# Moving the stationary operands of a float32r matmul chain to odd multiples of 32 bytes, modulo 512, from the moving operands

## The chip, the core and the metric

The kernel runs on one core of one Trainium2 chip. The metric is the device time of one execution in microseconds (us); shown are the median and the ends of three runs, and one further execution that the hardware profiler recorded. The engines are named as in the profile: PE is TensorE's matmuls, PEld its weight loads, DVE is VectorE, ACT is ScalarE, POOL is GpSimd, and SP issues most DMAs.

## The reference

The input x has 4 sequences of 1024 tokens with 1024 features, cut into 8 groups of 128. Everything is float32.

```
h  = einsum('btel,elf->btef', x.reshape(B, T, 8, 128), W1) + b1     # 8 experts, 128 -> 512
h  = gelu(h)
y  = einsum('btef,efl->btel', h, W2) + b2                           # 512 -> 128
eo = silu(cond) @ emb_W + emb_b                                     # one row per sequence
scale, shift = split(eo)
hn = layernorm(y.reshape(B, T, 1024), ln_g, ln_b) * (1 + scale) + shift
out = x + silu(hn) @ out_W + out_b                                  # 1024 -> 1024
```

## The kernel before

**Three products for one.** Every operand of a matmul is split into a high part, rounded to float32r, and a low part, the float32r rest. Each product then takes three matmuls: high by high, low by high, high by low. A matmul loads a stationary block of 128 columns (LDWEIGHTS) and streams a moving block of 512 columns past it. Each of the two halves of a 1024-token tile loads its block again, so loads and matmuls are equal in number.

**First stage (L907 to L946).** 32 items, one for each group g and each tile t of 1024 tokens. An item has four chunks of 128 hidden features. For a chunk, `first` (L928) multiplies a 128-column cut of W1 (stationary) with the transposed input `xT_hi`, `xT_lo` (moving) and `second` (L944) a cut of W2 (stationary) with the gelu's parts `g_hi`, `g_lo` (moving): 12 matmuls for a chunk, 48 for an item. PE runs `first` two chunks ahead of `second`. The parts of W1 and W2 of a group lie in one of `WS = 4` slots of the tensor `W` (slot g % 4, each 8 KB on a partition). ACT and DVE write them (L476, L634; the first group L539 to L654) from `wraw`, which the DMA fills.

**Second stage (L948 to L1021).** 16 pairs p of 128-token tiles. DVE, ACT and POOL take the layer norm of a pair and its silu; `round_s` on ACT (L519) writes the high part `s_hi[p % 2]`, `rest_s` on DVE (L800) the low part `s_lo[p % 2]`. In `project` (L954) the silu parts are the stationary operand, in cuts of 128 tokens, and the output weights `oW_hi`, `oW_lo` the moving one: 48 matmuls for a tile, 96 for a pair. The last tile is done in three pieces of 512, 256 and 256 columns (`project_pieces`, L1004: 24 matmuls of 512 columns and 48 of 256). "Pair 1" in the change stands for the buffers with index 1, which the odd pairs use; the even pairs, the first among them, use index 0.

**Order.** All engine programs are written out by hand and wait on semaphores; no scheduler moves an instruction. PE waits for the writers of its operands (`w_split`, `xhi_done`, `glo_done`, `slo_done`) and for the readers of its results (`y_staged`, `out_ready`).

**Places.** `at(name, shape, offset)` (L128) puts a tensor at a fixed byte of each partition, from `BASE = 33 * 512`. With S0 = 64 KB and R0 = S0 + 21 * 512, the matmuls' operands are placed by these lines:

```
oW_hi = at("oW_hi", [P, G, D], 0, F32R)
W = at("W", [P, WS, 4, FF], R0 + 16 * KB, F32R)
xT_hi = at("xT_hi", [P, 2, TA], R0 + 56 * KB, F32R)
g_hi = at("g_hi", [P, 2, TA], R0 + 80 * KB, F32R)
s_lo0 = at("s_lo0", [P, G, TP], R0 + 8 * KB, F32R)
s_hi1 = at("s_hi1", [P, G, TP], R0 + 16 * KB, F32R)
s_lo1 = at("s_lo1", [P, G, TP], R0 + 24 * KB, F32R)
s_hi0 = at("s_hi0", [P, G, TP], R0 + 124 * KB, F32R)
```

All of them start at multiples of 512 bytes. A stationary cut is 128 columns of 4 bytes, 512 bytes, and a moving half is 2048 bytes, so every operand of every matmul of the data starts at 0 modulo 512.

Of the kernel before, what the change touches and what calls it, by code (L numbers as in the profile page):

```python
# [15 lines left out]
def cond_ffn_program(nc, x, xT, vectors, cond, W1, W2, emb_T, out_W, out_b, out):  # L16
    B, T, D = x.shape
    G, L, FF = W1.shape
    C = FF // P
    NE = emb_T.shape[1]  # L20
    K = emb_T.shape[2]
    KH = K // 2
    TA = 2 * BANK
    NT = B * T // TA
    TP = 2 * P
# [6 lines left out]
    HG = G // 2  # L32
# [12 lines left out]
    WS = 4  # L45
# [12 lines left out]
    EARLY = 2  # L58
# [65 lines left out]
    with ExitStack() as ctx:  # L124
# [30 lines left out]


        emb_out = [at(f"emb_out{k}", [P, HG, K], (16 + 32 * k) * KB) for k in range(2)]
        emb_cols = [emb_out[k] if o is None else at(f"emb_cols{k}", [P, len(range(NE)[cut]), K], R0 + o * KB)
                    for k, (_, cut, o) in enumerate(PIECES)]


        cond_all = [at(f"cond_all{k}", [P, K], o) for k, o in enumerate((R0 + 128 * KB, S0 + 5632))]
        cond_tanh_all = at("cond_tanh_all", [P, EARLY, K], R0 + 104 * KB)
        dot_out = [at(f"dot_out{k}", [P, KH], S0 + 2 * k * KB) for k in range(2)]
        wraw = at("wraw", [P, 2, 2 * FF], R0 + 8 * KB)
        W = at("W", [P, WS, 4, FF], R0 + 16 * KB, F32R)
        xT_raw = at("xT_raw", [P, 2, TA], R0 + 48 * KB)
        xT_hi = at("xT_hi", [P, 2, TA], R0 + 56 * KB, F32R)
        xT_lo = at("xT_lo", [P, 2, TA], R0 + 64 * KB, F32R)
        g_raw = at("g_raw", [P, 2, TA], R0 + 72 * KB)  # L170
        g_hi = at("g_hi", [P, 2, TA], R0 + 80 * KB, F32R)
        g_lo = at("g_lo", [P, 2, TA], R0 + 88 * KB, F32R)
        y_stage = at("y_stage", [P, 2, TA], R0 + 96 * KB)

        yb0 = at("yb0", [P, G, TP], R0)
        tanh0 = at("tanh0", [P, G, TP], R0 + 8 * KB)
        s_lo0 = at("s_lo0", [P, G, TP], R0 + 8 * KB, F32R)
        s_hi1 = at("s_hi1", [P, G, TP], R0 + 16 * KB, F32R)
        s_lo1 = at("s_lo1", [P, G, TP], R0 + 24 * KB, F32R)
        res = at("res", [P, 4, D], R0 + 48 * KB)  # L180
        yb2 = at("yb2", [P, G, TP], R0 + 64 * KB)
        yb1 = at("yb1", [P, G, TP], R0 + 104 * KB)
        sq = at("sq", [P, G, TP], R0 + 112 * KB)
        out_b_all = at("out_b_all", [P, D], R0 + 120 * KB)
        s_hi0 = at("s_hi0", [P, G, TP], R0 + 124 * KB, F32R)
        tail_out = [at(f"tail_out{k}", [P, K], o) for k, o in enumerate((S0, R0 + 32 * KB))]
        tail_cond = at("tail_cond", [P, B - EARLY, K], R0 + 72 * KB)
        tail_cols = [at(f"tail_cols{k}", [P, K], R0 + o * KB) for k, o in enumerate((36, 40, 80, 84, 88, 92))]
        mean_part1 = at("mean_part1", [P, HG, TP], R0 + 124 * KB)
        yb = (yb0, yb1, yb2)  # L190
        s_hi = (s_hi0, s_hi1)
        s_lo = (s_lo0, s_lo1)
# [264 lines left out]
        def _(act):  # L457
# [7 lines left out]
            def round_raw(j):  # L465
                kind, g = LOADS[j]
                act.wait_ge(wraw_landed[j % 2], raw_count(j))
                if kind == "W" and g >= WS:
                    act.wait_ge(s2_done, C * (LAST_ITEM[g - WS] + 1))
                if kind == "O" and g >= HG:  # L470

                    act.wait_ge(emb_dot, 4 * (2 * (g - HG) + 1))
                for h in range(2):
                    half = slice(h * FF, (h + 1) * FF)
                    if kind == "W":
                        nc.scalar.copy(W[:, g % WS, 2 * h], wraw[:, j % 2, half]).then_inc(w_act_rounded, 1)  # L476
# [59 lines left out]
                round_s(0, h)  # L536

            act.wait_ge(w0_landed, 16)
            nc.scalar.copy(W[:, 0, W1_HI, 0:P], wraw[:, 0, 0:P]).then_inc(w0_rounded, 1)  # L539
            act.wait_ge(x0_landed[1], 16)  # L540
            nc.scalar.copy(xT_hi[:, 0, BANK:], xT_raw[:, 0, BANK:]).then_inc(xhi_done, 1)
            act.wait_ge(w1_landed, 16)
            nc.scalar.copy(W[:, 0, W1_HI, P:FF], wraw[:, 0, P:FF]).then_inc(w_rounded, 1)
            act.wait_ge(vec_landed, 16)
            gelu(0)
            gelu(1)
# [66 lines left out]
        def _(dve):  # L613
            nc.vector.memset(eps[:], LN_EPS).then_inc(eps_set, 1)

            def split_raw(j, h):
                kind, g = LOADS[j]
                half = slice(h * FF, (h + 1) * FF)
                raw = wraw[:, j % 2, half]
                if j == 0:  # L620

                    hi, lo = W[:, 0, W2_HI], W[:, 0, W2_LO]
                    dve.wait_ge(w2_landed, 16)
                    nc.vector.tensor_copy(hi, raw).then_inc(w_rounded, 1)
                    dve.wait_ge(w_rounded, 2)
                elif kind == "W":
                    hi, lo = W[:, g % WS, 2 * h], W[:, g % WS, 2 * h + 1]
                    dve.wait_ge(w_act_rounded, 2 * (g - 1) + h + 1)
                else:
                    hi, lo = oW_hi[:, g, half], oW_lo[:, g, half]  # L630
                    if g >= HG:
                        dve.wait_ge(emb_dot, 4 * (2 * (g - HG) + 2))
                    dve.wait_ge(o_rounded, 2 * g + h + 1)
                nc.vector.tensor_tensor(lo, raw, hi.bitcast(F32), ALU.subtract).then_inc(w_split, 1)  # L634
# [2 lines left out]
            dve.wait_ge(x0_landed[0], 16)  # L637
            nc.vector.tensor_copy(xT_hi[:, 0, 0:BANK], xT_raw[:, 0, 0:BANK]).then_inc(x0_hi, 1)
            dve.wait_ge(w0_rounded, 1)
            nc.vector.tensor_tensor(W[:, 0, W1_LO, 0:P], wraw[:, 0, 0:P], W[:, 0, W1_HI, 0:P].bitcast(F32),  # L640
                                    ALU.subtract).then_inc(w0_split, 1)

            def rest_x0(h):
# [5 lines left out]
            rest_x0(0)  # L649
            rest_x0(1)  # L650
            dve.wait_ge(w_rounded, 1)
            nc.vector.tensor_tensor(W[:, 0, W1_LO, P:FF], wraw[:, 0, P:FF], W[:, 0, W1_HI, P:FF].bitcast(F32),
                                    ALU.subtract).then_inc(w_split, 1)
            split_raw(0, 1)  # L654

# [250 lines left out]
        def _(pe):  # L906
            def first(m, low_part=None):  # L907
                n, c = divmod(m, C)
                g = ORDER[n][0]
                cut = slice(c * P, (c + 1) * P)  # L910
                if m == 2:
                    pe.wait_ge(gelu0_half, 1)
                if m >= 3:
                    pe.wait_ge(gelu_done, m - 1)
                parts = [(W1_HI, xT_hi), (W1_LO, xT_hi), (W1_HI, xT_lo)]
                if m == 1:

                    parts = [parts[0], parts[2], parts[1]]
                for k, (w, v) in enumerate(parts):
                    if m == 1 and k == 2:  # L920
                        pe.wait_ge(w_split, 1)
                    if k == 2 and low_part is not None:
                        pe.wait_ge(xlo_done, low_part)
                    for h in range(2):
                        half = slice(h * BANK, (h + 1) * BANK)
                        if (m, k, h) == (2, 0, 1):
                            pe.wait_ge(gelu_done, 1)
                        mm = nc.tensor.matmul(ring(m)[:, half], W[:, g % WS, w, cut], v[:, n % 2, half],  # L928
                                              start=(k == 0), stop=(k == 2))
                mm.then_inc(s1_done, 1)  # L930

            def second(m):
                n, c = divmod(m, C)
                g = ORDER[n][0]
                cut = slice(c * P, (c + 1) * P)
                if c == 0 and n >= 2:
                    pe.wait_ge(y_staged, n - 1)
                pe.wait_ge(ghi_act if act_rounds(m) else ghi_dve, ROUNDED[m])
                for k, (w, v) in enumerate(((W2_HI, g_hi), (W2_LO, g_hi), (W2_HI, g_lo))):
                    if k == 2:  # L940
                        pe.wait_ge(glo_done, m + 1)
                    for h in range(2):
                        half = slice(h * BANK, (h + 1) * BANK)
                        mm = nc.tensor.matmul(y_psum(n)[:, half], W[:, g % WS, w, cut], v[:, m % 2, half],  # L944
                                              start=(c == 0 and k == 0), stop=(c == C - 1 and k == 2))
                mm.then_inc(s2_done, 1)  # L946

# [17 lines left out]
            for k, h in ((0, 0), (1, 0), (0, 1), (1, 1), (2, 0), (2, 1)):  # L965
# [7 lines left out]
                    pe.wait_ge(w0_split, 1)  # L973
                if k == 2:
                    pe.wait_ge(xlo_done if h else x0_lo, 1)
                mm = nc.tensor.matmul(ring(0)[:, half], W[:, 0, w, 0:P], v[:, 0, half],  # L976
                                      start=(k == 0), stop=(k == 2))
            mm.then_inc(s1_done, 1)
            pe.wait_ge(w_rounded, 1)
# [76 lines left out]
```

## Time and profile before

| | us |
|---|---|
| median of three runs (lowest, highest) | 706.69 (706.60, 706.92) |
| the profiled execution | 707.23 |
| its span, first to last instruction | 705.2 |
| PE busy, 3100 matmuls | 701.7 |
| PEld busy, 3100 loads | 579.7 |
| DVE busy | 603.1 |
| ACT busy | 469.9 |
| POOL busy | 104.1 |
| DMA queues of SP: share of the 16 engines' span | 47.0% |

Matmuls are pipelined: a 512-column matmul is recorded with 389 ns, but the next one starts before it ends. What a matmul costs PE is therefore the distance from its start to the next start, and not its recorded duration. The chain of waits gives that distance directly: it lists pieces of the chain with their start, their length and the number of instructions in them.

### The profile page before, as it was taken

Reading aid. Unit: us, or ns where it says so; the run is one execution under the profiler, and the core shown is the slowest. Engines: PE = TensorE matmul, PEld = TensorE weight load, DVE = VectorE, ACT = ScalarE, POOL = GpSimd, SP = SyncE. Lnnn points to the kernel's source line nnn. Section 1 sums busy time; section 2 is a strip of 40 time slices with the busy share of each in tenths; the row PEclk is TensorE's granted clock in tenths of the full one; section 3 lists DMA queues with packets and bytes.
Section 4 is the critical chain, followed back from the end, with each engine's and each line's share of the span. In section 5 each row is a group of like instructions: output and inputs, shape, how many; then the busy total and the mean of one; then the engine's idle time right before and its main releaser. Section 6 shows DMA issues by size and latency. Waiting matters only on the chain.

```text
span 705.2 us, 8337 instructions
## 1 busy us (share of the span) xinstructions
PE 701.7 (100%) x3100; PEld 579.7 (82%) x3100; DVE 603.1 (86%) x724; ACT 469.9 (67%) x527; POOL 104.1 (15%) x68
## 2 busy tenths in 40 slices
PE   9999999999999999999999999999999999999998
PEld 6888888888888888888888888888888888888887
DVE  6888999999999889899887999999999978677511
ACT  6898888888878779898883456454656464555500
POOL 0000000000000011100121332323232432322100
PEclk9999999999999999999999999999999999999999
DMA  7676566354332631333789687888698877565531
GB/s 240 232 246 204 182 210 220 110 178 139 101 120 81 217 120 60 120 102 108 206 288 290 197 278 236 272 247 252 220 293 267 257 217 210 184 173 146 153 120 59
DMA packets 51880, 133.22 MB, mean 189 GB/s; under 512 B 4096, under 2 KB 25216, under 8 KB 49408
## 3 DMA queue, kind: packets, MB, share of 16 engines
q1 hardware_dynamic: 46944, 115.79, 47.0%
q0 software_dynamic: 4608, 16.78, 12.3%
q8 instruction: 24, 0.39, 0.2%
q10 hardware_dynamic: 288, 0.13, 0.1%
q14 instruction: 16, 0.13, 0.1%
HBM read 82.35 MB, written 33.55 MB: 164 GB/s over the span
## 4 chain that ended last, share of the span: by engine, by line
PE 100%; DVE 0%; DVEq 0%; issue 0%
PE psum L954 48%; PE psum L944 25%; PE psum L928 25%; PE psum L1004 2%; PE psum L962 1%; PE psum L976 0%; DVE res L902 0%; DVEq L124 0%
## 5 line engine op out<-in xcount | busy, mean ns | idle before, releaser
L672 DVE TENSOR_TENSOR g_lo<-g_raw,g_hi 128x1024 fp32r<-128x1024 f32 x128 | 158.4, 1239 | 27.7 <-ACT g_hi L500 24.9
L494 ACT ACTIVATE g_raw<-psum,cols 128x1024 f32<-128x1024 f32 x127 | 141.8, 1117 | 34.7 <-PE psum L928 28.0
L954 PE MATMUL psum<-oW_hi,s_hi 128*128 128x512 f32 x496 | 152.7, 389 | 0.0
L954 PE MATMUL psum<-oW_hi,s_lo 128*128 128x512 f32 x496 | 152.7, 389 | 0.0
L954 PE MATMUL psum<-oW_lo,s_hi 128*128 128x512 f32 x496 | 152.6, 389 | 0.0
L944 PE MATMUL psum<-g_hi,W 128*128 128x512 f32 x512 | 136.9, 389 | 0.0
L928 PE MATMUL psum<-xT_hi,W 128*128 128x512 f32 x508 | 135.9, 389 | 0.0
L944 PEld LDWEIGHTS psum<-g_hi,W 128*128 128x128 f32 x512 | 96.1, 188 | 20.0
L928 PEld LDWEIGHTS psum<-xT_hi,W 128*128 128x128 f32 x508 | 95.3, 188 | 20.1 <-ACT g_raw L490 0.2
L954 PEld LDWEIGHTS psum<-oW_hi,s_hi 128*128 128x128 f32 x496 | 93.1, 188 | 19.4
L954 PEld LDWEIGHTS psum<-oW_hi,s_lo 128*128 128x128 f32 x496 | 93.1, 188 | 19.3
L954 PEld LDWEIGHTS psum<-oW_lo,s_hi 128*128 128x128 f32 x496 | 93.1, 188 | 19.3
L594 ACT ACTIVATE yb<-yb,mod_c,mod_a 128x256 f32<-128x256 f32 x120 | 62.3, 590 | 56.6 <-DVE yb L782 56.6
L424 POOL PARTITION_ALL_REDUCE mean_all<-mean_total x16 | 41.2, 2578 | 385.2 <-DVE mean_total L755 385.2
L944 PE MATMUL psum<-g_lo,W 128*128 128x512 f32 x256 | 78.8, 389 | 0.0
L875 DVE TENSOR_TENSOR res<-psum,res 128x1024 f32<-128x1024 f32 x31 | 37.8, 1218 | 47.5 <-PE psum L954 47.5
L928 PE MATMUL psum<-xT_lo,W 128*128 128x512 f32 x254 | 78.2, 389 | 0.0
L500 ACT CAST g_hi<-g_raw 128x1024 fp32r<-128x1024 f32 x63 | 66.2, 1051 | 8.5 <-PE psum L944 7.2
L514 ACT ACTIVATE sq<-yb 128x1024 f32<-128x1024 f32 x32 | 34.0, 1063 | 36.6 <-DVE yb L760 35.6
L431 POOL PARTITION_ALL_REDUCE var_all<-var_total x16 | 35.8, 2239 | 142.4 <-DVE var_total L773 142.4
L705 DVE SCALAR_TENSOR_TENSOR tail_out<-tail_cols,tail_cond 128x1024 f32<-128x1024 f32 x32 | 52.4, 1666 | 4.7 <-DMA tail_cols<-in_emb_T 4.6
L944 PEld LDWEIGHTS psum<-g_lo,W 128*128 128x128 f32 x256 | 48.0, 188 | 10.1 <-DVE g_lo L672 0.2
(77 smaller groups left out, 688.5 us busy)
## 6 DMA issues: line engine op xcount, KB each, us to landing
y_scratch<-y_stage SPq DMA_DIRECT2D x32, 512.0 KB, 3.1
yb<-y_scratch SPq DMA_DIRECT2D x16, 1024.0 KB, 4.8
res<-in_x SPq DMA_DIRECT2D x32, 512.0 KB, 6.0
res<-out_b_all POOLq DMA_DIRECT2D x32, 512.0 KB, 4.5
xT_raw<-in_xT SPq DMA_DIRECT2D x31, 512.0 KB, 4.5
out<-res SPq DMA_DIRECT2D x31, 512.0 KB, 4.1
tail_cols<-in_emb_T SPq DMA_DIRECT2D x24, 512.0 KB, 7.1
wraw<-in_out_W SPq DMA_DIRECT2D x16, 256.0 KB, 4.9
```

The source lines that it names most:

```text
L424: nc.gpsimd.partition_all_reduce(mean_all[:], mean_total[:], P, bass.bass_isa.ReduceOp.add).then_inc(mean_done, 1)
L431: nc.gpsimd.partition_all_reduce(var_all[:], var_total[:], P, bass.bass_isa.ReduceOp.add).then_inc(var_done, 1)
L494: nc.scalar.activation(g_raw[:, m % 2], ring(m), ACT.Gelu, bias=cols[:, R_B1 + k:R_B1 + k + 1]).then_inc(gelu_done, 1)
L500: nc.scalar.copy(g_hi[:, m % 2], g_raw[:, m % 2]).then_inc(ghi_act, 1)
L514: nc.scalar.activation(sq[:, half_of(h)], yb[p % 3][:, half_of(h)], ACT.Square).then_inc(squared, 1)
L594: nc.scalar.activation(yb[p % 3][:, g], yb[p % 3][:, g], ACT.Silu, scale=mod_a[:, b, g:g + 1], bias=mod_c[:, b, g:g + 1]).then_inc(silu_do ...
L672: nc.vector.tensor_tensor(g_lo[:, m % 2], g_raw[:, m % 2], g_hi[:, m % 2].bitcast(F32), ALU.subtract).then_inc(glo_done, 1)
L705: nc.vector.scalar_tensor_tensor(tail_out[i % 2][:], tail_cols[l % SLOTS][:], 1.0, tail_cond[:, b - EARLY], ALU.mult, ALU.mult, accum_out= ...
L875: nc.vector.tensor_tensor(res[:, q % 4], proj(q), res[:, q % 4], ALU.add).then_inc(out_ready, 1)
L928: mm = nc.tensor.matmul(ring(m)[:, half], W[:, g % WS, w, cut], v[:, n % 2, half], start=(k == 0), stop=(k == 2))
L944: mm = nc.tensor.matmul(y_psum(n)[:, half], W[:, g % WS, w, cut], v[:, m % 2, half], start=(c == 0 and k == 0), stop=(c == C - 1 and k == 2))
L954: mm = nc.tensor.matmul(proj(q)[:, half], v[:, g, cut], w[:, g, half], start=(g == 0 and k == 0), stop=(g == G - 1 and k == 2))
```

## The change

The tensors change places. No instruction is added, taken away or put elsewhere: the instruction streams of all engines are the same, row for row. `W` becomes four tensors, one for each slot, that begin at 32, 96, 288 and 480 bytes modulo 512. Buffer 1 of the silu parts begins at 32 (`s_hi1`) and 96 (`s_lo1`). These six places are odd multiples of 32 bytes. Whatever lies behind `W` moves up by 512 bytes to make room, and so stays at 0 modulo 512: the moving operands, and `s_hi0`. `s_lo0` and `wraw` stay where they were.

```
-        W = at("W", [P, WS, 4, FF], R0 + 16 * KB, F32R)
-        xT_raw = at("xT_raw", [P, 2, TA], R0 + 48 * KB)
-        xT_hi = at("xT_hi", [P, 2, TA], R0 + 56 * KB, F32R)
...
+        W = [at(f"W{s}", [P, 4, FF], R0 + (16 + 8 * s) * KB + o, F32R) for s, o in enumerate((32, 96, 288, 480))]
+        xT_raw = at("xT_raw", [P, 2, TA], R0 + 48 * KB + 512)
+        xT_hi = at("xT_hi", [P, 2, TA], R0 + 56 * KB + 512, F32R)
...
         s_lo0 = at("s_lo0", [P, G, TP], R0 + 8 * KB, F32R)
-        s_hi1 = at("s_hi1", [P, G, TP], R0 + 16 * KB, F32R)
-        s_lo1 = at("s_lo1", [P, G, TP], R0 + 24 * KB, F32R)
...
+        s_hi1 = at("s_hi1", [P, G, TP], R0 + 16 * KB + 32, F32R)
+        s_lo1 = at("s_lo1", [P, G, TP], R0 + 24 * KB + 96, F32R)
...
-        s_hi0 = at("s_hi0", [P, G, TP], R0 + 124 * KB, F32R)
...
+        s_hi0 = at("s_hi0", [P, G, TP], R0 + 124 * KB + 512, F32R)
...
-                        mm = nc.tensor.matmul(ring(m)[:, half], W[:, g % WS, w, cut], v[:, n % 2, half],
+                        mm = nc.tensor.matmul(ring(m)[:, half], W[g % WS][:, w, cut], v[:, n % 2, half],
```

## Rows read from the trace of the kernel before

**Rows 1.** The page, parts 1 and 2: busy time by engine, granted clock in 40 slices.
```profile
PE 701.7 (100%) x3100; PEld 579.7 (82%) x3100; DVE 603.1 (86%) x724; ACT 469.9 (67%) x527; POOL 104.1 (15%) x68
...
PEclk9999999999999999999999999999999999999999
```

**Rows 2.** The page, part 4: the chain that ended last, by line.
```profile
PE psum L954 48%; PE psum L944 25%; PE psum L928 25%; PE psum L1004 2%; PE psum L962 1%; PE psum L976 0%; DVE res L902 0%; DVEq L124 0%
```

**Rows 3.** Waits of engine PE: engine, line <- releaser: us, times, longest.
```profile
PE psum L962 <- PEq L1046: 0.8, 1, 0.8
```

**Rows 4.** The chain in order of time: start us, length us, line, instructions.
```profile
53.39 1.36 PE psum L944 x6
...
355.37 335.92 PE psum L954 x1482
691.29 11.20 PE psum L1004 x72
```

**Rows 5.** Timeline of PE in the last pieces, 256 columns: start us, length us.
```profile
699.32 0.28 PE L1004 MATMUL psum<-oW_hi,s_lo 128*128 128x256 f32 x1
699.44 0.28 PE L1004 MATMUL psum<-oW_hi,s_hi 128*128 128x256 f32 x1
```

**Rows 6.** Groups by line and form, PE and PEld: count, busy us, mean ns, idle us.
```profile
L944 PE MATMUL psum<-g_hi,W 128*128 128x512 f32 x512 | 136.9, 389 | 0.0
L928 PE MATMUL psum<-xT_hi,W 128*128 128x512 f32 x508 | 135.9, 389 | 0.0
L944 PE MATMUL psum<-g_lo,W 128*128 128x512 f32 x256 | 78.8, 389 | 0.0
L928 PE MATMUL psum<-xT_lo,W 128*128 128x512 f32 x254 | 78.2, 389 | 0.0
L954 PE MATMUL psum<-oW_hi,s_hi 128*128 128x512 f32 x496 | 152.7, 389 | 0.0
...
L944 PEld LDWEIGHTS psum<-g_hi,W 128*128 128x128 f32 x512 | 96.1, 188 | 20.0
```

**Rows 7.** The chain near the start: start us, length us, line, instructions.
```profile
9.81 1.39 PE psum L944 x6
11.20 1.39 PE psum L928 x6
12.59 1.36 PE psum L944 x6
```

**Rows 8.** Timeline of PE, first matmuls of the data: start us, length us.
```profile
5.67 0.63 PE L976 MATMUL psum<-xT_hi,W 128*128 128x512 f32 x1
6.10 0.85 PE L976 MATMUL psum<-xT_lo,W 128*128 128x512 f32 x2
```

**Rows 9.** Writers of the moved tensors: groups of ACT and DVE.
```profile
L476 ACT CAST W<-wraw 128x512 fp32r<-128x512 f32 x14 | 7.9, 617 | 0.0
...
L634 DVE TENSOR_TENSOR W<-wraw,W 128x512 fp32r<-128x512 f32 x15 | 10.3, 685 | 0.0
...
L800 DVE TENSOR_TENSOR s_lo<-yb,s_hi 128x1024 fp32r<-128x1024 f32 x32 | 38.9, 1216 | 2.2 <-ACT s_hi L519 2.2
```

**Rows 10.** Stretches: PE, PEld, DVE, ACT, POOL busy us (instructions), granted clock, DMA share, GB/s.
```profile
20.00:100.00 80.00, 80.00 (x355) 66.26 (x354) 71.63 (x94) 70.28 (x75) 0.00 (x0) 1.00 0.67 227
100.00:250.00 150.00, 150.00 (x664) 124.24 (x663) 141.88 (x217) 126.24 (x128) 0.00 (x0) 1.00 0.43 143
250.00:345.00 95.00, 95.00 (x420) 78.55 (x419) 86.16 (x97) 81.53 (x79) 9.12 (x6) 1.00 0.35 115
...
400.00:550.00 150.00, 150.00 (x664) 124.20 (x663) 148.74 (x158) 79.60 (x105) 48.73 (x29) 1.00 0.83 257
```

More of the change, by code:

```diff
@@ L157, in cond_ffn_program @@
         emb_out = [at(f"emb_out{k}", [P, HG, K], (16 + 32 * k) * KB) for k in range(2)]
-        emb_cols = [emb_out[k] if o is None else at(f"emb_cols{k}", [P, len(range(NE)[cut]), K], R0 + o * KB)
+        emb_cols = [emb_out[k] if o is None else at(f"emb_cols{k}", [P, len(range(NE)[cut]), K], R0 + o * KB + (512 if o else 0))
                     for k, (_, cut, o) in enumerate(PIECES)]
-        cond_all = [at(f"cond_all{k}", [P, K], o) for k, o in enumerate((R0 + 128 * KB, S0 + 5632))]
-        cond_tanh_all = at("cond_tanh_all", [P, EARLY, K], R0 + 104 * KB)
+        cond_all = [at(f"cond_all{k}", [P, K], o) for k, o in enumerate((R0 + 128 * KB + 512, S0 + 5632))]
+        cond_tanh_all = at("cond_tanh_all", [P, EARLY, K], R0 + 104 * KB + 512)
         dot_out = [at(f"dot_out{k}", [P, KH], S0 + 2 * k * KB) for k in range(2)]
         wraw = at("wraw", [P, 2, 2 * FF], R0 + 8 * KB)
-        W = at("W", [P, WS, 4, FF], R0 + 16 * KB, F32R)
-        xT_raw = at("xT_raw", [P, 2, TA], R0 + 48 * KB)
-        xT_hi = at("xT_hi", [P, 2, TA], R0 + 56 * KB, F32R)
[L169 to L173, printed above, removed]
+        W = [at(f"W{s}", [P, 4, FF], R0 + (16 + 8 * s) * KB + o, F32R) for s, o in enumerate((32, 96, 288, 480))]
+        xT_raw = at("xT_raw", [P, 2, TA], R0 + 48 * KB + 512)
+        xT_hi = at("xT_hi", [P, 2, TA], R0 + 56 * KB + 512, F32R)
+        xT_lo = at("xT_lo", [P, 2, TA], R0 + 64 * KB + 512, F32R)
+        g_raw = at("g_raw", [P, 2, TA], R0 + 72 * KB + 512)
+        g_hi = at("g_hi", [P, 2, TA], R0 + 80 * KB + 512, F32R)
+        g_lo = at("g_lo", [P, 2, TA], R0 + 88 * KB + 512, F32R)
+        y_stage = at("y_stage", [P, 2, TA], R0 + 96 * KB + 512)
         yb0 = at("yb0", [P, G, TP], R0)
@@ L177, in cond_ffn_program @@
         s_lo0 = at("s_lo0", [P, G, TP], R0 + 8 * KB, F32R)
-        s_hi1 = at("s_hi1", [P, G, TP], R0 + 16 * KB, F32R)
-        s_lo1 = at("s_lo1", [P, G, TP], R0 + 24 * KB, F32R)
[L180 to L184, printed above, removed]
-        s_hi0 = at("s_hi0", [P, G, TP], R0 + 124 * KB, F32R)
[L186 to L189, printed above, removed]
+        s_hi1 = at("s_hi1", [P, G, TP], R0 + 16 * KB + 32, F32R)
+        s_lo1 = at("s_lo1", [P, G, TP], R0 + 24 * KB + 96, F32R)
+        res = at("res", [P, 4, D], R0 + 48 * KB + 512)
+        yb2 = at("yb2", [P, G, TP], R0 + 64 * KB + 512)
+        yb1 = at("yb1", [P, G, TP], R0 + 104 * KB + 512)
+        sq = at("sq", [P, G, TP], R0 + 112 * KB + 512)
+        out_b_all = at("out_b_all", [P, D], R0 + 120 * KB + 512)
+        s_hi0 = at("s_hi0", [P, G, TP], R0 + 124 * KB + 512, F32R)
+        tail_out = [at(f"tail_out{k}", [P, K], o) for k, o in enumerate((S0, R0 + 32 * KB + 512))]
+        tail_cond = at("tail_cond", [P, B - EARLY, K], R0 + 72 * KB + 512)
+        tail_cols = [at(f"tail_cols{k}", [P, K], R0 + o * KB + 512) for k, o in enumerate((36, 40, 80, 84, 88, 92))]
+        mean_part1 = at("mean_part1", [P, HG, TP], R0 + 124 * KB + 512)
         yb = (yb0, yb1, yb2)
@@ L475, in round_raw @@
                     if kind == "W":
-                        nc.scalar.copy(W[:, g % WS, 2 * h], wraw[:, j % 2, half]).then_inc(w_act_rounded, 1)
+                        nc.scalar.copy(W[g % WS][:, 2 * h], wraw[:, j % 2, half]).then_inc(w_act_rounded, 1)
                     else:
@@ L538, in _ @@
             act.wait_ge(w0_landed, 16)
-            nc.scalar.copy(W[:, 0, W1_HI, 0:P], wraw[:, 0, 0:P]).then_inc(w0_rounded, 1)
+            nc.scalar.copy(W[0][:, W1_HI, 0:P], wraw[:, 0, 0:P]).then_inc(w0_rounded, 1)
             act.wait_ge(x0_landed[1], 16)
@@ L542, in _ @@
             act.wait_ge(w1_landed, 16)
-            nc.scalar.copy(W[:, 0, W1_HI, P:FF], wraw[:, 0, P:FF]).then_inc(w_rounded, 1)
+            nc.scalar.copy(W[0][:, W1_HI, P:FF], wraw[:, 0, P:FF]).then_inc(w_rounded, 1)
             act.wait_ge(vec_landed, 16)
@@ L620, in split_raw @@
                 if j == 0:
-                    hi, lo = W[:, 0, W2_HI], W[:, 0, W2_LO]
+                    hi, lo = W[0][:, W2_HI], W[0][:, W2_LO]
                     dve.wait_ge(w2_landed, 16)
@@ L626, in split_raw @@
                 elif kind == "W":
-                    hi, lo = W[:, g % WS, 2 * h], W[:, g % WS, 2 * h + 1]
+                    hi, lo = W[g % WS][:, 2 * h], W[g % WS][:, 2 * h + 1]
                     dve.wait_ge(w_act_rounded, 2 * (g - 1) + h + 1)
@@ L639, in _ @@
             dve.wait_ge(w0_rounded, 1)
-            nc.vector.tensor_tensor(W[:, 0, W1_LO, 0:P], wraw[:, 0, 0:P], W[:, 0, W1_HI, 0:P].bitcast(F32),
+            nc.vector.tensor_tensor(W[0][:, W1_LO, 0:P], wraw[:, 0, 0:P], W[0][:, W1_HI, 0:P].bitcast(F32),
                                     ALU.subtract).then_inc(w0_split, 1)
@@ L651, in _ @@
             dve.wait_ge(w_rounded, 1)
-            nc.vector.tensor_tensor(W[:, 0, W1_LO, P:FF], wraw[:, 0, P:FF], W[:, 0, W1_HI, P:FF].bitcast(F32),
+            nc.vector.tensor_tensor(W[0][:, W1_LO, P:FF], wraw[:, 0, P:FF], W[0][:, W1_HI, P:FF].bitcast(F32),
                                     ALU.subtract).then_inc(w_split, 1)
@@ L943, in second @@
                         half = slice(h * BANK, (h + 1) * BANK)
-                        mm = nc.tensor.matmul(y_psum(n)[:, half], W[:, g % WS, w, cut], v[:, m % 2, half],
+                        mm = nc.tensor.matmul(y_psum(n)[:, half], W[g % WS][:, w, cut], v[:, m % 2, half],
                                               start=(c == 0 and k == 0), stop=(c == C - 1 and k == 2))
@@ L975, in _ @@
                     pe.wait_ge(xlo_done if h else x0_lo, 1)
-                mm = nc.tensor.matmul(ring(0)[:, half], W[:, 0, w, 0:P], v[:, 0, half],
+                mm = nc.tensor.matmul(ring(0)[:, half], W[0][:, w, 0:P], v[:, 0, half],
                                       start=(k == 0), stop=(k == 2))
```

## The prediction, before the changed kernel was run

> **What bounds the kernel now.** I read the page's busy times first: PE is busy for 701.7 of 705.2 us, at the granted clock's full level, 2.4 GHz, in all 40 slices [rows 1]. The chain that ended last is matmuls alone, 98% of it in the three lines of the data [rows 2], and PE's only recorded wait is 0.8 us at the very start [rows 3]. So the time is the number of matmuls by the distance between their starts, and only a change of that distance can move it.
>
> The chain in order of time gives the distance. 1482 matmuls of the second stage take 335.92 us, 226.67 ns each; six matmuls of the first stage take 1.36 us, the same [rows 4]. 512 columns at 2.4 GHz are 213.33 ns, so **13.3 ns** of each matmul are not streaming. In the last pieces the starts stand 0.12 us apart for 256 columns, which stream in 106.7 ns [rows 5]: the excess is 13.3 ns again, whatever the width. It goes with the matmul, or with the weight load that each matmul has.
>
> **The change, part by part.** Nothing is added or taken away; every engine's instructions keep their order. What differs is where the bytes lie.
>
> *Stationary operands of the first stage.* 512 + 508 + 256 + 254 matmuls of L944 and L928 [rows 6] and 6 of L976, together 1536, load from `W`, whose four slots go from 0 to 32, 96, 288 and 480 modulo 512, while the moving side stays at 0. *Stationary operands of the odd pairs.* Seven odd pairs with 96 matmuls and the last with 48 + 72 make 792. The even pairs' 768 keep their relation. So 1536 + 792 = 2328 matmuls, three quarters, get a new distance between the two addresses, and each nanosecond of spacing on them is worth 2.3 us.
>
> What does the new distance cost or give for each matmul? No row shows a matmul at another distance: all stand at 0 modulo 512. I bound it by the nearest rows. Below: the spacing cannot fall under the streaming time, so at most 13.3 ns go, 2328 * 13.3 = 31.0 us. Above: the slowest spacing at full clock without a wait on the path is that of the two pieces from 9.81 to 12.59 us, 12 matmuls in 2.78 us, 231.7 ns [rows 7], 5.0 ns more than later; 2328 * 5.0 = 11.6 us. Between the ends I take **0**, the row with 1482 matmuls at one spacing. Its moving operands come from 64 KB of `oW_hi` and `oW_lo` and its stationary ones from four buffers in different corners of the partition, DVE, ACT and DMA load comes and goes over it, and the spacing does not follow any of this. That looks like a fixed price of swapping a float32r weight block, not like two streams that meet in the memory.
>
> The Trainium skill, SBUF — State Buffer, section "Who interferes with whom", gives TensorE one read port for the moving operand and an independent one for LDWEIGHTS. By that the distance between the two addresses is worth nothing and the sum stays 706.7; no row here can show the ports themselves.
>
> *Weight loads.* At 32 modulo 512 each 512-byte cut lies across a 512-byte boundary. A load lasts 188 ns and its queue idles 20.0 us over 512 loads, 39 ns each [rows 6]; in the last pieces loads of the same block keep up with a spacing of 0.12 us [rows 5]. A load could so take up to 39 ns longer before a 512-column matmul waits for it. Without that cover each nanosecond more would again cost 2.3 us. I take 0.
>
> *Writers.* ACT writes a half slot in 617 ns and DVE its rest in 685, DVE the low silu half in 1216 [rows 9]. Only these touch the moved stationary tensors besides PE; no DMA does. PE has waited for none of them in the rows, so tens of nanoseconds on some 60 instructions stay off the path: 0. *Tensors moved by 512 bytes.* Same place modulo 512, same DMA sizes: 0.
>
> The sum is 0. The profiled execution took 707.23 us, 2.0 more than its span, and stands 0.5 above the median of 706.69; so the median stays at **706.7**, and a profiled run near 707.2.
>
> **The rivals.**
>
> *Faster: the 13.3 ns are a collision between the weight load and the moving stream, and an odd distance avoids it.* For it: the excess is no constant of the matmul. Between 9.8 and 12.6 us the same form takes 231.7 ns [rows 7], and the first matmuls start 0.43 us apart [rows 8], which is 512 columns at 1.2 GHz, the lower level, with nothing over: when the stream asks for half as many bytes, the excess is gone. Also, one load brings 512 bytes for either width, as the equal excess wants. Against it: no jitter over hundreds of microseconds.
>
> Its price, if the whole excess goes, is not 31.0 us, because DVE becomes the bound. From 20 to 345 us it is busy 71.63 + 141.88 + 86.16 = 299.7 of 325 us, 92%, and 95% between 100 and 250 [rows 10], while PE would shrink to 94% (213.3 / 226.7). Of the first stage's 1536 * 13.3 = 20.5 us I count three quarters, 15.4. In the second stage the odd pairs' 792 * 13.3 = 10.6 us include some 331 matmuls (4.4 us) between 400 and 550 us, where DVE is busy for 148.74 of 150 us [rows 10] and leaves 1.3; so 10.6 - 3.1 = 7.5. Together 22.9, which gives **683.8**. If only some of the six places avoid it, or each half: **695**.
>
> The Trainium skill, TensorE: Matmul & The Clock Gate, section "Back-to-back issue gap", gives columns / 2.4 + 2.5 ns, 215.8 for 512. The trace shows 226.7, so it does not agree for these operands; if the page's spacing came out on the 2328 matmuls, the estimate from it is 2328 * 10.8 = 25 us before DVE binds.
>
> *Slower: the equal places are the good case.* With stationary and moving cuts in step the pattern has settled at 226.67; before it settles it runs at 231.7 [rows 7], with the same instructions and the same places. If an odd distance keeps the two from falling into step, every moved matmul takes 231.7: 706.7 + 11.6 = **718.3**. It decides at once, since PE has no slack: 0.6 ns on the moved matmuls are 1.4 us, 0.2% of the time, which is about what a measurement of this kernel can tell from no change. Against it: nothing in rows 7 says that the places are what settles.
>
> *The change does not reach the mechanism:* the excess depends on the places, but by another distance or another modulus than these. That gives 706.7 too, and is counted with the forecast.
>
> **How the numbers follow.** No effect (with the last case): 0.46. Collision avoided: 0.32, half of it in part (690 to 701, where 690 is three quarters of 22.9) and half of it whole (some 684). Slower: 0.22, nearly all of it up to 718.3. The range takes the forecast, the slower side and the partial gain: 0.46 + 0.20 + 0.16 = 0.82, from **690** to **719**; the whole gain is what I leave out. Faster by over 0.2%: 0.32; within: 0.46; slower: 0.22. The likeliest case alone would be 706.2 to 707.2.
>
> **What would show it.** In the chain of the changed kernel the 1482 matmuls of the second stage should still take 335.9 us and six of the first stage 1.36. If the rivals hold, the second stage alternates, one pair at 96 * 226.67 = 21.76 us and the next at another length, and the items of one slot differ from those of another: slot by slot the first stage is its own comparison. If the faster rival holds, PE also gets its first waits for DVE (`glo_done`, `out_ready`), and loads of 188 ns may shorten. A second stage that is slower in even pairs as well would tell against all three, since nothing changed there.

## The result, and the profile after

The changed kernel takes **721.65 us** (721.04 to 721.85), the kernel before 706.81 us beside it: a ratio of **1.0206, 95% interval 1.0193 to 1.0218**. It is slower by 14.8 us. The forecast was 706.7 with a range up to 719: the sign of the "slower" rival came true, and by more than its price.

The page of the changed kernel, busy times, granted clock and the chain by line, against [rows 1] and [rows 2]:

```profile
PE 716.0 (99%) x3100; PEld 579.0 (80%) x3100; DVE 605.1 (84%) x724; ACT 471.7 (66%) x527; POOL 104.1 (14%) x68
...
PEclk9999999999999999999999999999999999999999
...
PE psum L955 47%; PE psum L945 25%; PE psum L929 24%; PE psum L1005 2%; DMA wraw<-in_W 1%; SPq L334 0%; DVE g_hi L671 0%; DVE W L625 0%; SPq L336 0%; SPq L335 0%; DVE res L903 0%; DVEq L124 0%; DVE W L635 0%
```

(Line numbers are one higher than before.) PE is as full as before, at the same granted clock, with as many matmuls; the DMA and the short pieces of DVE and SPq in the chain lie in the first 10 us or behind the last matmul. The weight loads' own busy time has not grown: 579.0 us against 579.7. PE's recorded waits after the start are one of 0.3 us:

```profile
PE psum L963 <- PEq L1047: 0.8, 1, 0.8
PE psum L945 <- DVE g_hi L671: 0.3, 1, 0.3
```

So the matmuls themselves stand further apart. The chain in order of time (start us, length us, line, instructions):

```profile
12.79 1.40 PE psum L945 x6
...
365.58 340.29 PE psum L955 x1482
705.86 11.24 PE psum L1005 x72
```

Against [rows 4] and [rows 7] this splits the loss. The start costs 0.20 us (12.79 against 12.59, the same piece). From there to the block of 1482, 1512 matmuls of 226.67 ns took 342.78 us; now the same stretch takes 365.58 - 12.79 = 352.79, **10.01 us more, 6.6 ns for each**. The 1482 matmuls take **4.37 us more**; 720 of them belong to odd pairs, 6.1 ns for each if those carry all of it. The last pieces take 0.04 more. Together 14.62; the span went from 705.2 to 719.9.

The second stage holds a comparison within one kernel, since only the odd pairs moved. The timeline of PE in the first even pair, buffers at distance 0 (start us, length us):

```profile
379.95 0.61 PE L955 MATMUL psum<-oW_hi,s_lo 128*128 128x512 f32 x2
...
382.67 0.61 PE L955 MATMUL psum<-oW_hi,s_lo 128*128 128x512 f32 x2
```

and in the odd pair behind it, buffers at 32 and 96:

```profile
394.68 0.63 PE L955 MATMUL psum<-oW_lo,s_hi 128*128 128x512 f32 x2
...
398.40 0.63 PE L955 MATMUL psum<-oW_hi,s_hi 128*128 128x512 f32 x2
```

Twelve matmuls in 2.72 us are 226.7 ns each; sixteen in 3.72 us are 232.5, 5.8 more. The instruction and the moving operand are the same.

The first stage has one slot of `W` in each of four stretches. Matmuls that fall into each (a matmul is recorded with 0.39 us, so its spacing is the length plus 0.39, divided by the count; one matmul more or less is 1.8 ns):

```profile
20.00:48.00 28.00, 28.00 (x122) 1.00 0.86 285
60.00:90.00 30.00, 30.00 (x129) 1.00 0.50 173
103.00:133.00 30.00, 30.00 (x131) 1.00 0.51 166
149.00:179.00 30.00, 30.00 (x130) 1.00 0.37 116
```

The kernel before has 125, 134, 134 and 134 there. The counts say that all four odd multiples lose, but they can't tell the four from each other. The chain can: in each stretch it lists pieces of six matmuls, and the time between the starts of two pieces that lie far apart, divided by the matmuls between them, gives the spacing to 0.2 ns or better. The first two lines are from the kernel before (126 matmuls from one start to the other, 226.7 ns), the others from the changed kernel, slots at 32 (114 matmuls, 233.3) and at 96 (120, 234.3):

```profile
60.19 1.36 PE psum L928 x6
88.75 1.36 PE psum L944 x6
...
19.79 1.40 PE psum L929 x6
46.39 1.40 PE psum L945 x6
...
60.41 1.41 PE psum L945 x6
88.52 1.41 PE psum L945 x6
```

The slots at 288 and 480 have 233.3 ns too. The counts of the four stretches, in this order of slots, are quoted below for the experiments; the spacings in ns are read from the chain in this way.

### The profile page after: what moved, and what is told of

Read it like the earlier page. It is cut to its first block, busy times and chain, and to the rows that moved or that the text cites. A ratio compares the mean times of both kernels' runs of the same rounds, so it can differ in the third digit from the quotient of the medians.

```text
span 719.9 us, 8337 instructions
## 1 busy us (share of the span) xinstructions
PE 716.0 (99%) x3100; PEld 579.0 (80%) x3100; DVE 605.1 (84%) x724; ACT 471.7 (66%) x527; POOL 104.1 (14%) x68
## 4 chain that ended last, share of the span: by engine, by line
PE 98%; DMA 1%; SPq 0%; DVE 0%; issue 0%; DVEq 0%
PE psum L955 47%; PE psum L945 25%; PE psum L929 24%; PE psum L1005 2%; DMA wraw<-in_W 1%; SPq L334 0%; DVE g_hi L671 0%; DVE W L625 0%; SPq L336 0%; SPq L335 0%; DVE res L903 0%; DVEq L124 0%; DVE W L635 0%
## 5 line engine op out<-in xcount | busy, mean ns | idle before, releaser
L945 PE MATMUL psum<-g_hi,W 128*128 128x512 f32 x512 | 140.4, 396 | 0.3 <-DVE g_hi L671 0.3
L929 PE MATMUL psum<-xT_hi,W 128*128 128x512 f32 x508 | 139.2, 395 | 0.0
L945 PE MATMUL psum<-g_lo,W 128*128 128x512 f32 x256 | 80.5, 396 | 0.0
L929 PE MATMUL psum<-xT_lo,W 128*128 128x512 f32 x254 | 79.9, 395 | 0.0
L929 PEld LDWEIGHTS psum<-xT_lo,W 128*128 128x128 f32 x254 | 47.7, 188 | 11.5
```

What stands on the lines that cost most here:

```text
L929: mm = nc.tensor.matmul(ring(m)[:, half], W[g % WS][:, w, cut], v[:, n % 2, half], start=(k == 0), stop=(k == 2))
L945: mm = nc.tensor.matmul(y_psum(n)[:, half], W[g % WS][:, w, cut], v[:, m % 2, half], start=(c == 0 and k == 0), stop=(c == C - 1 and k == 2))
```

## The experiments

After the result the theory was that the **distance** between stationary and moving operand sets the spacing. Its first rival was that the **place** of the stationary cut does, because it lies across a 512-byte boundary. The edits are shown against the changed kernel; `...` marks lines left out.

**e1_all_by_32.** All tensors 32 bytes further, and all distances back at 0.

```
-        BASE = 33 * 512
+        BASE = 33 * 512 + 32
...
-        W = [at(f"W{s}", [P, 4, FF], R0 + (16 + 8 * s) * KB + o, F32R) for s, o in enumerate((32, 96, 288, 480))]
+        W = [at(f"W{s}", [P, 4, FF], R0 + (16 + 8 * s) * KB + o, F32R) for s, o in enumerate((0, 0, 0, 0))]
...
+        s_hi1 = at("s_hi1", [P, G, TP], R0 + 16 * KB + 0, F32R)
+        s_lo1 = at("s_lo1", [P, G, TP], R0 + 24 * KB + 0, F32R)
```

> The kernel with every stationary operand back at 0 modulo 512 from the moving ones, and all tensors, moving ones too, 32 bytes further: every operand of every matmul begins at 32 modulo 512, at distance 0. Theory (distance): what counts is the distance between the stationary and the moving operand, so all 3096 matmuls keep 226.67 ns and the time is 706.8 us. Rival (place): what counts is that a stationary cut lies across a 512-byte boundary (or begins off a multiple of 64), so all 3096 matmuls are slow, the even pairs too: 721.65 + 768 * 5.7 ns = 726 us.

Measured: 707.12 us, ratio to before 1.0003 (0.9994 to 1.0013). The four stretches hold 125, 134, 134 and 134 matmuls, and the second stage is that of before:

```profile
355.29 335.92 PE psum L955 x1482
```

Lying across a 512-byte boundary costs nothing; the rival falls.

**e2_moving_by_32.** The mirror image: as e1, but with `W` and the odd pairs' parts 480 bytes further, so that they stand at 0 and the moving operands at 32.

```
+        BASE = 33 * 512 + 32
...
+        W = [at(f"W{s}", [P, 4, FF], R0 + (16 + 8 * s) * KB + o, F32R) for s, o in enumerate((480, 480, 480, 480))]
...
+        s_hi1 = at("s_hi1", [P, G, TP], R0 + 16 * KB + 480, F32R)
+        s_lo1 = at("s_lo1", [P, G, TP], R0 + 24 * KB + 480, F32R)
```

> All tensors 32 bytes further as in e1_all_by_32, but W and the silu parts of the odd pairs at 0 modulo 512 again: there the moving side is at 32 and the stationary side at 0, distance 480. In the even pairs both are at 32, distance 0. Theory (distance): the first stage and the odd pairs are slow (about 1.40 us for six matmuls, 22.3 us for an odd pair), the even pairs keep 226.67 ns: about 721 us. Rival (place of the stationary cut): the other way round, the first stage at 1.36 us for six, odd pairs 21.76 us, even pairs 22.3: 706.8 + 768 * 5.7 ns = 711 us.

Measured: 721.69 us, ratio 1.0210 (1.0195 to 1.0225). The stretches hold 122, 130, 130 and 131. In the chain:

```profile
365.12 340.76 PE psum L955 x1482
```

The timeline of an even pair (first two lines) and of the odd pair behind it:

```profile
379.94 0.62 PE L955 MATMUL psum<-oW_hi,s_hi 128*128 128x512 f32 x2
...
382.66 0.62 PE L955 MATMUL psum<-oW_hi,s_hi 128*128 128x512 f32 x2
...
399.86 0.63 PE L955 MATMUL psum<-oW_lo,s_hi 128*128 128x512 f32 x2
...
403.59 0.63 PE L955 MATMUL psum<-oW_hi,s_hi 128*128 128x512 f32 x2
```

Modulo 512 the stationary operands of the first stage and of the odd pairs lie where they lay in the kernel before, and they are slow (sixteen matmuls of an odd pair in 3.73 us, 233.1 ns); in the even pairs both operands lie at 32, and twelve matmuls take 2.72 us, 226.7 ns each. The distance decides, not the place.

**e3_even_multiples.** `W` at 64, 128, 192, 256, the odd pairs at 384, the even pairs at 64.

```
+        W = [at(f"W{s}", [P, 4, FF], R0 + (16 + 8 * s) * KB + o, F32R) for s, o in enumerate((64, 128, 192, 256))]
...
+        s_lo0 = at("s_lo0", [P, G, TP], R0 + 8 * KB + 64, F32R)
+        s_hi1 = at("s_hi1", [P, G, TP], R0 + 16 * KB + 384, F32R)
+        s_lo1 = at("s_lo1", [P, G, TP], R0 + 24 * KB + 384, F32R)
...
+        s_hi0 = at("s_hi0", [P, G, TP], R0 + 124 * KB + 576, F32R)
```

> Distances that are even multiples of 32: the four slots of W at 64, 128, 192 and 256, the silu parts of the odd pairs at 384, of the even pairs at 64. Theory with a pattern of two places of 32 bytes: even multiples meet just as equal places do, every stretch keeps 1.36 us for six and the time is 706.8 us. Theory with a longer pattern: the slots differ from each other, some at 1.40 or more, between 707 and 727 us. Rival (any place off 512 is slow): all six slow, 721.65 + 4.4 = 726 us.

Measured: 721.91 us, ratio 1.0212 (1.0192 to 1.0232).

```profile
102.93 1.37 PE psum L929 x6
131.77 1.37 PE psum L945 x6
...
149.54 1.36 PE psum L929 x6
176.74 1.36 PE psum L929 x6
...
360.88 345.09 PE psum L955 x1482
```

Oddness is not what costs: 64 and 128 are slow, with 233.3 and 232.4 ns, and so are the pairs, 9.17 us over 335.92. But the slots differ: 192 has 228.9 ns (first two lines, 126 matmuls from start to start), and 256 has 226.7 (next two, 120 matmuls), as 0 has.

**e4_other_odd.** `W` at 160, 224, 352, 416, the odd pairs at 448, the even pairs at 128.

```
+        W = [at(f"W{s}", [P, 4, FF], R0 + (16 + 8 * s) * KB + o, F32R) for s, o in enumerate((160, 224, 352, 416))]
...
+        s_lo0 = at("s_lo0", [P, G, TP], R0 + 8 * KB + 128, F32R)
+        s_hi1 = at("s_hi1", [P, G, TP], R0 + 16 * KB + 448, F32R)
+        s_lo1 = at("s_lo1", [P, G, TP], R0 + 24 * KB + 448, F32R)
...
+        s_hi0 = at("s_hi0", [P, G, TP], R0 + 124 * KB + 640, F32R)
```

> The four odd multiples that the change leaves out in W: 160, 224, 352 and 416; the odd pairs at 448 and the even pairs at 128, both even multiples. Theory with a pattern of two places: all slots of W slow at about 1.40 us for six, both kinds of pairs at 226.67 ns: 706.8 + 1536 * 6.7 ns = 717 us. Theory with a longer pattern: the slots differ, and pairs at 448 and 128 need not be at 226.67; one of them may even lie under it.

Measured: 723.71 us, ratio 1.0237 (1.0217 to 1.0258); stretches 122, 130, 130 and 131, the second stage 342.60 us for 1482. All odd multiples are slow: 233.3 ns at 160, 224 and 416, 234.3 at 352. No pair lies under 226.67 ns here. The surprise is in the last tile, whose buffers are at 448: its 72 matmuls take 10.95 us instead of 11.20, and those of 256 columns start 1.02 us / 9 = 113.3 ns apart, where [rows 5] have 120 (e12_search_lower, below, has another value at this distance):

```profile
715.94 0.28 PE L1005 MATMUL psum<-oW_hi,s_hi 128*128 128x256 f32 x1
...
716.96 0.28 PE L1005 MATMUL psum<-oW_hi,s_hi 128*128 128x256 f32 x1
```

**e5_few_bytes.** `W` at 4, 8, 16 and 24 bytes, cut out of a slightly larger tensor; the odd pairs at 320.

```
+        W = [at(f"W{s}", [P, 4 * FF + 8], R0 + (16 + 8 * s) * KB + o // 32 * 32, F32R)[:, o % 32 // 4:o % 32 // 4 + 4 * FF]
+             .rearrange("p (w f) -> p w f", w=4) for s, o in enumerate((4, 8, 16, 24))]
...
+        s_hi1 = at("s_hi1", [P, G, TP], R0 + 16 * KB + 320, F32R)
+        s_lo1 = at("s_lo1", [P, G, TP], R0 + 24 * KB + 320, F32R)
```

> Distances under 32 bytes: the slots of W at 4, 8, 16 and 24, the odd pairs at 320, the even pairs at 0. Theory (distance, read in lines of 32 bytes or more): all four slots act like 0, about 1.36 us for six, the odd pairs are slow at 320 (about 22.3 us), 706.8 + 4 = 711 us. Rival (distance by the column): slots differ already here and are slow, up to 1.40: 721 us. If one of them lies under 1.36, a better place than 0 exists.

Measured: 719.23 us, ratio 1.0176 (1.0147 to 1.0206). Stretches 122, 132, 131, 132: 232.3 ns at 4 bytes, 230.7 at 8, 233.3 at 16 and 230.0 at 24. One column of 4 bytes is enough, so the theory of lines of 32 bytes falls. The 1482 take 340.91 us: the odd pairs at 320 are slow.

**e6_just_under.** The same with other numbers, and the odd pairs at 256.

```
+             .rearrange("p (w f) -> p w f", w=4) for s, o in enumerate((488, 496, 504, 508))]
...
+        s_hi1 = at("s_hi1", [P, G, TP], R0 + 16 * KB + 256, F32R)
+        s_lo1 = at("s_lo1", [P, G, TP], R0 + 24 * KB + 256, F32R)
```

> Distances just under 512: the slots of W at 488, 496, 504 and 508 (24, 16, 8 and 4 bytes before the moving operand's place), the odd pairs at 256, where a slot of the first stage had 227.6 ns. Theory (distance in lines): all four slots begin in the line that begins at 480, so they act like 480 (1.40 us for six), odd pairs at 21.85 us: 717 us. Rival (distance by the column): 504 and 508 act like 0, 488 like 480.

Measured: 711.76 us, ratio 1.0069 (1.0046 to 1.0092).

```profile
60.43 1.37 PE psum L930 x6
87.83 1.37 PE psum L930 x6
...
103.12 1.40 PE psum L946 x6
131.12 1.40 PE psum L946 x6
...
149.00 1.36 PE psum L930 x6
177.56 1.36 PE psum L946 x6
...
359.53 335.92 PE psum L956 x1482
```

All lines are from the chain: slots at 496 and 504 (120 matmuls from start to start) and at 508 (126). So 488 has 231.1 ns, 496 228.3, 504 233.3 and 508 226.7; the odd pairs at 256 run exactly as before (last line). Neither theory says this: 508 acts like 0, but its neighbour 504 is among the slowest.

**e7_smaller_loads.** Distance 0 everywhere. In one of the three products the load has 64 columns (first stage) or 32 (second stage); the rest of that product is left out.

```
+                        rows = 64 if k == 1 else P
+                        mm = nc.tensor.matmul(ring(m)[0:rows, half], W[g % WS][:, w, c * P:c * P + rows], v[:, n % 2, half],
...
+                        rows = 32 if k == 1 else P
+                        mm = nc.tensor.matmul(proj(q)[0:rows, half], v[:, g, q % 2 * P:q % 2 * P + rows], w[:, g, half],
```

> All places back at distance 0, and smaller weight loads in the second of the three products (low part of W by high part, or high part of silu by low part of the output weights): 64 columns instead of 128 in the first stage, 32 in the second; the rest of that product is left out, so the output lacks it. The streamed columns stay 512. Theory (the 13.3 ns are the price of the bytes loaded beside the stream): they fall with the load, 6.7 ns for 64 columns and 3.3 for 32, so six matmuls of the first stage take 1.347 us and the second stage 1482 * (2 * 226.67 + 216.67) / 3 = 331.0 us instead of 335.9: 706.8 - 1020 * 6.7 / 2 ns - 5 = 698 us. Rival (a fixed price of swapping weights): no change, 706.8 us.

Measured: 714.94 us, ratio 1.0116 (1.0086 to 1.0145), slower than with whole loads. Groups of loads, then two pieces of the chain:

```profile
L958 PEld LDWEIGHTS psum<-oW_hi,s_hi 128*128 128x128 f32 x496 | 93.1, 188 | 20.5
L958 PEld LDWEIGHTS psum<-oW_lo,s_hi 128*32 128x32 f32 x496 | 53.5, 108 | 38.7
```

```profile
100.21 1.38 PE psum L947 x6
...
359.65 339.21 PE psum L958 x1482
```

The short loads last 108 ns instead of 188, and the matmuls are not nearer but further apart. A price for the bytes loaded would have brought 331.0 us, a fixed price 335.92. Both fall in this form. That the short loads break the steady rhythm is a reading, and not a thing that this run shows by itself: it also left out half or three quarters of that product's stationary columns, and with them its output rows.

**e8_own_or_running.** W1 and the transposed input both at 64, W2 and the gelu's parts both at 0.

```
+                self.a = at(f"W1s{s}", [P, 2, FF], R0 + (32 + 4 * s) * KB + 64, F32R)
+                self.b = at(f"W2s{s}", [P, 2, FF], R0 + (16 + 4 * s) * KB, F32R)
...
+        xT_hi = at("xT_hi", [P, 2, TA], R0 + 56 * KB + 64, F32R)
+        xT_lo = at("xT_lo", [P, 2, TA], R0 + 64 * KB + 64, F32R)
...
+        s_hi1 = at("s_hi1", [P, G, TP], R0 + 16 * KB + 0, F32R)
+        s_lo1 = at("s_lo1", [P, G, TP], R0 + 24 * KB + 0, F32R)
```

> Which stream counts, the matmul's own moving operand or the one that runs while its weights load. W1 and the transposed input both begin at 64 modulo 512, W2 and the gelu's parts both at 0, the second stage all at 0: every matmul has distance 0 to its own moving operand. A load runs beside the stream of the matmul before it; that has another distance (64 or 448) only where L928 and L944 follow each other, 2 loads of 12. Theory (own): nothing changes, 706.8 us. Theory (running stream): the first stage leaves its rhythm twice in 12 matmuls and spends some of the time between at 229 to 233 ns: 1536 * 2 to 5 ns more, 710 to 714.5 us, second stage unchanged at 335.9 us for 1482.

Measured: 712.58 us, ratio 1.0079 (1.0059 to 1.0099). The second stage takes 335.92 us for 1482; six matmuls of the first stage take 1.38, and 120 of them 27.67 (second line to third):

```profile
102.24 1.38 PE psum L938 x6
103.62 1.38 PE psum L954 x6
...
131.29 1.38 PE psum L954 x6
...
360.85 335.92 PE psum L964 x1482
```

Every matmul has distance 0 to its own moving operand, and yet the first stage is slow: 230.6 ns, 3.9 more on the average of all twelve. So the distance to the own moving operand is not what counts, or not alone. The distance to the stream that runs while the weights load fits, with two such loads in twelve. But at the same two places in twelve the moving stream itself jumps by 64 bytes, and so do the weights, and no run moves the streams without that; so this cause is likely, not shown.

**e9_all_at_256.** The change with another number: slots and both kinds of pairs at 256.

```
+        W = [at(f"W{s}", [P, 4, FF], R0 + (16 + 8 * s) * KB + o, F32R) for s, o in enumerate((256, 256, 256, 256))]
...
+        s_lo0 = at("s_lo0", [P, G, TP], R0 + 8 * KB + 256, F32R)
+        s_hi1 = at("s_hi1", [P, G, TP], R0 + 16 * KB + 256, F32R)
+        s_lo1 = at("s_lo1", [P, G, TP], R0 + 24 * KB + 256, F32R)
...
+        s_hi0 = at("s_hi0", [P, G, TP], R0 + 124 * KB + 768, F32R)
```

> The change with another number: all four slots of W and the silu parts of both kinds of pairs at 256 modulo 512. Theory (only some distances keep the 226.67 ns rhythm, 256 is one): odd pairs had 226.67 in e6_just_under and a slot 227.6 in e3_even_multiples, so 706.8 to 708.3 us. Rival (any shift off the moving operand's place costs): 721.65 + 768 * 5.7 ns = 726 us.

Measured: 706.86 us, ratio 0.9997 (0.9988 to 1.0007); stretches 126, 134, 134 and 134, and

```profile
355.55 335.92 PE psum L955 x1482
```

The same tensors moved by a similar amount, and the even pairs' with them, cost nothing. It was not the moving, but the places.

**e10_w_only.** The change without its second part.

```
+        s_hi1 = at("s_hi1", [P, G, TP], R0 + 16 * KB + 0, F32R)
+        s_lo1 = at("s_lo1", [P, G, TP], R0 + 24 * KB + 0, F32R)
```

> The change in its first half alone: the slots of W at 32, 96, 288 and 480 as in the change, the silu parts of the odd pairs back at 0. If the cost is the sum of the moved matmuls, the first stage keeps its 10.2 us and the second loses 4.4: 721.65 - 4.4 = 717.2 us, with 335.9 us for the 1482 matmuls. Rival (the slow first stage sets off something that the second pays for): the second stage stays above 338 us.

Measured: 716.93 us, ratio 1.0141 (1.0125 to 1.0156); stretches 121, 130, 130 and 130, and in the chain

```profile
11.99 1.40 PE psum L945 x6
...
364.78 335.95 PE psum L955 x1482
```

The two parts are independent. The first stage takes the 352.79 us from its piece at 11.99 to the block, as it does in the changed kernel from 12.79, and the block of 1482 is back at 335.95.

**e11_around_256.** `W` at 240, 248, 252 and 260, the odd pairs at 256.

```
+             .rearrange("p (w f) -> p w f", w=4) for s, o in enumerate((240, 248, 252, 260))]
...
+        s_hi1 = at("s_hi1", [P, G, TP], R0 + 16 * KB + 256, F32R)
+        s_lo1 = at("s_lo1", [P, G, TP], R0 + 24 * KB + 256, F32R)
```

> Does 256 behave as 0 does? In e6_just_under the cost falls column by column towards 0 (488: 233, 496: 231, 504: 228.5, 508: 226.7 ns), and 4 bytes past 0, in e5_few_bytes, it is back at 232. Here the slots of W are at 240, 248, 252 and 260, the odd pairs at 256, the even pairs at 0. Theory (the pattern repeats after 256 bytes): 231, 228.5, 226.7 and 232 ns, 30 us windows with 132, 133, 134 and 131 matmuls, pairs unchanged at 335.9 us for 1482: about 712 us. Rival (256 is an accident of one place): the neighbours are all at 231 to 234: 716 us.

The expectation has the values of 488, 496 and 504 in the wrong order, so that the cost seems to fall evenly towards 0; e6's are those given above. Measured: 712.16 us, ratio 1.0071 (1.0048 to 1.0093); stretches 125, 131, 134 and 131. Slots at 248 and 252, 120 matmuls from start to start:

```profile
60.49 1.40 PE psum L930 x6
88.49 1.40 PE psum L930 x6
...
103.61 1.36 PE psum L946 x6
130.81 1.36 PE psum L946 x6
```

That is 233.3 and 226.7 ns; 240 has 226.7 and 260 has 232.4. Set beside the distances 256 bytes further, 248 agrees with 504 (233.3), 252 with 508 (226.7) and 260 with 4 (232.3); 240 does not agree with 496 (228.3). The other runs have more such pairs, all alike within 0.2 ns: 0 and 256, 32 and 288, 64 and 320, 96 and 352, 160 and 416, 188 and 444, 192 and 448, 224 and 480. So the pattern repeats after 256 bytes, except for 240 and 496, and between its ends it is jagged. The distance is not the whole of it either: 128 has 232.4 ns in the first stage (e3) and 233.3 in the even pairs of e4.

**e12_search_lower.** `W` at 184, 188, 444 and 452, the odd pairs at 448.

```
+             .rearrange("p (w f) -> p w f", w=4) for s, o in enumerate((184, 188, 444, 452))]
...
+        s_hi1 = at("s_hi1", [P, G, TP], R0 + 16 * KB + 448, F32R)
+        s_lo1 = at("s_lo1", [P, G, TP], R0 + 24 * KB + 448, F32R)
```

> Looks for a distance under 226.67 ns: the slots of W at 184, 188, 444 and 452, around the two even multiples that lay lowest besides 0 and 256 (192 at 229.3, 448 at 228.9), the odd pairs at 448, the even pairs at 0. If 0 and 256 are the lowest points of the pattern, no stretch lies under 1.36 us for six, and the time is 710 to 715 us. If a lower rhythm exists near 192 or 448 (the last pieces of e4_other_odd, 256 columns at distance 448, took 113 ns each where distance 0 takes 120), a slot falls under 1.36, to 1.32 at most by that step of 6.7 ns, and a 30 us window holds up to 138 matmuls.

Measured: 718.02 us, ratio 1.0148 (1.0119 to 1.0178); stretches 122, 131, 130 and 130 (232.0 ns at 184, 233.3 at the other three), and 337.53 us for 1482, which is 2.2 ns more on each of the 720 at 448. No stretch of 512-column matmuls lies under 226.67 ns, at any distance tried. No version beats the kernel before.

The last tile has its buffers at 448, as in e4, but its 256-column matmuls do not repeat e4's 113.3 ns: 26 of them take 3.06 us, 117.7 ns each.

```profile
709.88 0.28 PE L1006 MATMUL psum<-oW_lo,s_hi 128*128 128x256 f32 x1
...
712.94 0.28 PE L1006 MATMUL psum<-oW_hi,s_hi 128*128 128x256 f32 x1
```

So the same operands at the same distance can run at two spacings; what chooses between them is open. Both are under the 120 ns of distance 0, and so are the last pieces of the other runs that left 0 there: 117.9 in the changed kernel (32 and 96), 116.7 in e2 (480), 118.7 in e3 (384) and 117.8 in e5 (320). At 256 (e6, e9) they have 120.

## Why the prediction was wrong

**Right: the bound, and what a nanosecond is worth.** PE is 98% of the chain or more, before and after, and all but 0.2 us of the loss is spacing. With 2328 moved matmuls, 14.8 us are 6.4 ns for each.

**Right: weight loads, writers and the tensors moved by 512 bytes cost nothing.** PEld's busy time is unchanged, e1 shows the cut across a boundary to be free, and e9, with the same writers writing to moved tensors, takes 706.86 us.

**Wrong: the term for the distance, "between the ends I take 0".** The argument was that the 1482 matmuls keep one spacing over many buffers, so that the spacing "looks like a fixed price". But all those buffers lay at distance 0 modulo 512; the row showed that nothing that varied in it mattered, and could not show that the distance didn't. e1, e2 and e9 show that it does: 0 is free with all operands 32 bytes further, 256 is free in both stages, and 480 costs as much (233.3 ns) when the moving side is shifted as when the stationary side is. The Trainium skill's separate ports for the two operands (SBUF — State Buffer, section "Who interferes with whom") agreed with the zero, and no run shows the ports themselves; the measured spacing depends on the two addresses all the same, so here the measurement decides.

**Wrong: the upper end.** The price was 5.0 ns, from the 12 matmuls of [rows 7], and the range ended there, at 719. Measured are 6.6 ns in the first stage and 5.8 to 6.1 in the odd pairs; a few early matmuls on their way to the rhythm are no ceiling for matmuls that never find it. The 48 matmuls of 256 columns, which the 2328 include, did not lose at all. With the measured prices the slower rival comes out at 706.8 + 10.0 + 4.4 + 0.2 = 721.4.

**The slower rival came true in its sign, and its mechanism in part.** It said that equal places let the two fall into step at 226.67 ns and that other places keep them from it. The even pairs of the changed kernel do run at 226.7. But the good places are not the equal ones alone (252, 256 and 508 are as good), and at 256 columns the equal places are the slow case. "In step" is a picture that fits; no run shows what the two do in the memory.

**The faster rival fell for 512 columns.** No distance of those tried brings a 512-column matmul under 226.67 ns. Some of its signs were right: the excess is no constant, and at 256 columns distance 0 is the slow case (120 ns against 113.3 to 118.7), but that is only 48 of the 3100 matmuls. Another sign, 0.43 us at the lower clock level, was read from the spacing alone: the trace's record of the granted clock begins at 6.57 us, at full speed, behind those matmuls.

**Open:** what in the memory or the array makes 0, 252, 256 and 508 good and 4, 248 and 504 bad, and what the 13.3 ns at distance 0 consist of. e7 shows only that they did not shrink when some of the loads did. The commonest slow spacing, 233.3 ns, has an excess of 20.0 ns over 213.3, and 113.3 ns at 256 columns one of 6.7: by this arithmetic one and a half times the 13.3, and half of them. That looks like steps of a fixed size; the values between show that it isn't all.

## What to carry to other kernels

Where float32r matmuls of 512 columns fill the time, the byte at which the weights begin, counted from the moving operands, is a parameter of the kernel: keep it at 0 (or 256) modulo 512 for all operands, the moving ones of different products too, since e8 lost 0.8% where two products stood apart. For 256 columns 0 is not the best place in these runs, and it has to be measured. Read the spacing from the chain (the starts of pieces far apart, divided by the matmuls between them), not from the busy share, which stayed at 99% through a loss of 2%. And a row in which a quantity never varied is no bound on what it costs when it does.

## What the runs showed of the hardware

- The spacing of 512-column float32r matmuls depends on the distance modulo 512 between the stationary and the moving operands: 226.7 ns at 0, 240, 252, 256 and 508; 228.3 to 228.9 at 192, 448 and 496; 230.0 to 232.5 at 4, 8, 24, 184, 260, 384 and 488; 232.4 or 233.3 at 128; 233.3 at 16, 32, 64, 160, 188, 224, 248, 288, 320, 416, 444, 452, 480 and 504; 234.3 at 96 and 352. Four bytes of difference can cost 6.6 ns (504 and 508).
- Moving all operands together by 32 bytes costs nothing (1.0003), though every cut then lies across a 512-byte boundary.
- Distance 0 to each matmul's own moving operand is not enough: with the two products of the first stage 64 bytes apart its matmuls took 230.6 ns (1.0079).
- Smaller weight loads made the matmuls slower (1.0116): loads of 32 columns end after 108 ns instead of 188, and the second stage goes from 226.7 to 228.9 ns.
- At 256 columns the excess over streaming is 13.3 ns at distances 0 and 256, and less at the others tried: 6.7 (e4) and 11.0 (e12) at 448, 10.0 at 480 (spacings of 120, 113.3, 117.7 and 116.7 ns).
